# Scan products ahead of the output projection, one decay-difference pair on VectorE, and conv taps laid apart, in a Mamba-2 layer's step loop

## The chip, the cores and the metric

The kernel runs on one core of a Trainium2 chip. The metric is the time of one execution on the device in microseconds (us); lower is better. TensorE (PE, with PEld its weight loads), VectorE (DVE), ScalarE (ACT), GpSimd (POOL) and the DMA queue of SyncE (SP) run their own instruction streams in order and meet only at semaphores.

## The reference, cut to what matters

A decoder layer: a Mamba-2 block, then cross attention, then a mixture-of-experts block, each behind a LayerNorm. The change lies in the Mamba-2 block alone. Its input is 8 sequences of 256 tokens with 256 channels, and it has 64 heads of 64 channels (4096 inner channels).

```python
proj = x_normed @ W_in.T                 # z (4096), x (4096), B and C (128 each), dt (64)
xBC = silu(causal_conv(xBC, 4 taps) + conv_b)
dt = softplus(dt + dt_bias);  dA = dt * -exp(A_log)
# per head: decay from token s to token l is exp(cum_l - cum_s), cum being the running sum of dA
Y = sum over s <= l of (C_l . B_s) * exp(cum_l - cum_s) * dt_s * x_s
y = Y + D * x
g = y * silu(z);  out = rmsnorm(g) * norm_w @ W_out.T
```

## The kernel before

The tokens are cut into 4 groups of 512 (two sequences each, `BG` = 2), and the inner channels into 32 tiles of 128 (`NCT`), which hold two heads each (`HPT` = 2). A step `n` is one tile of one group: 128 steps (`N`), group by group. Each engine has a loop over the steps, written out by hand; there is no planner. While a group runs, the loops also prepare the next group (`prepare_next`: B, C, dt, the running sums, normalised and transposed tokens), a few instructions in most steps.

What one step does, with the lines of the profile:

- TensorE: `transposes(n)` turns the conv output (L1049), `x_proj(n + 2)` and `z_proj(n + 1)` project ahead, 6 products each (L1021), `prepare_next`, then `out_proj(n - 1)` (L1078) and `scan(n)` (L1062), the products of the masked decays with x dt. In the steps called `turned` (the second of a group, and the last), `scan(n)` stands ahead of `out_proj(n - 1)`.
- ScalarE, in this order: `scale_x(n + 1)` (conv tap 0 with bias, L503), `gaps(n + 2)` (L517 and L520: for each of 2 heads and 2 sequences, a 128x256 and a 128x128 activation that form max(cum - cum', 0) of a pair of rows; four pairs), `tanh_x(n + 1)` (L536), `square(n - 1)` (L532), `tanh_z(n + 1)` (L542), `prepare_next`, `decays(n + 2)` (the exponential of all differences, L526).
- VectorE: `gate(n - 1)` (L791, waits for the scan), `x_times_dt(n)` (L779, waits for the transposes), `conv_x(n + 1)` (L749: taps 1 to 3, each added to the same tile and each waiting for the one before; tap 1 waits for `scale_x(n + 1)`), `prepare_next`, `matrices(n + 1)` (L761), `silu_x(n + 1)` (L766), `silu_z(n + 1)` (L773).
- GpSimd: `matrices_off(n + 1)` (L387, after `matrices(n + 1)`), `product(n)` (L396, after `gate(n)`), `add_square(n - 1)` (L407). For the first 28 steps it also splits weights, `w_high(n + 4)` (L367) ahead of `product(n)` and `w_low(n + 4)` (L374) behind it.
- SP: `a_load(k + 5)` (running sums, broadcast to all partitions, L282), which waits for the gaps three steps earlier, then `w_load(k + 4)` (L265).

`tanh_x(n + 1)` waits for all taps of `conv_x(n + 1)`; what stands behind it on ScalarE waits with it, up to `scale_x(n + 2)` of the next round of the loop.

Of the kernel before, what the change touches and what calls it, by code (L numbers as in the profile page):

```python
# [9 lines left out]
ALU = mybir.AluOpType  # L10
ACT = mybir.ActivationFunctionType
AX_X = mybir.AxisListType.X

P = 128
# [6 lines left out]
TPG = TG // P  # L21
# [41 lines left out]
def mamba_phase(nc, xres, ident, raw, banks, scratch, tiny, xT, next_loads, keys, split, x, w_xz, w_bc, w_dt, conv_w, conv_b, dt_bias, a_log, d_param, norm_w,  # L63
# [5 lines left out]
    NCT = w_xz.shape[1]  # L69
    HD = 64  # L70
    HPT = P // HD
    NH = NCT * HPT
    CB = 2
    SEQ = 256
    BG = TG // SEQ
    TAPS = conv_w.shape[-1]
    CONV = TAPS - 1
    EPS = 1e-5
    N = NG * NCT
# [3 lines left out]
    EARLY = 2 * TPG  # L83
    WO_ACT = NCT - 12
    SOFT = 3 + len(LOG1P)
    numbers = []

    with ExitStack() as ctx:
# [3 lines left out]
        def sem(name):  # L92
            s = ctx.enter_context(nc.semaphore("m_" + name))
            numbers.append(s.num)
            return s
# [7 lines left out]
        cw = sb("cw", [P, conv_w.shape[1], TAPS])  # L103
# [5 lines left out]
        cum = sb("cum", [P, 2 * TPG, NH])  # L109
# [15 lines left out]
        a_all = [sb(f"a_all{u}", [P, HPT, TG])[:] for u in range(3)]  # L125
# [12 lines left out]
        late = raw[:, RING * XZ:]  # L138
# [3 lines left out]
        aT = late[:, (CB + 1) * TG:(CB + 1) * TG + SEQ]  # L142
# [9 lines left out]
        def pb(name, banks=1):  # L152
# [4 lines left out]
        ps_y, ps_s = pb("ps_y"), pb("ps_s")  # L157
# [25 lines left out]
            sem(n) for n in ("x_ready", "z_ready", "t_ready", "y_ready", "out_ready", "sum_ready"))  # L183
        (x_scaled, gap_done, exp_done, x_tanh, z_tanh, g_squared) = (
            sem(n) for n in ("x_scaled", "gap_done", "exp_done", "x_tanh", "z_tanh", "g_squared"))
        mat_off = sem("mat_off")
        (conv_step, x_silu, z_silu, xdt_done, mat_done, gy_done, g_done, sum_mean, x_added) = (
            sem(n) for n in ("conv_step", "x_silu", "z_silu", "xdt_done", "mat_done", "gy_done", "g_done",
                             "sum_mean", "x_added"))
# [36 lines left out]
        def first_rows(u, h, b):  # L226
            at = (h * BG + b) * 2 * P
            pair = mat[:, u, at:].rearrange("p (j t) -> p j t", t=P)
            step = (2 * HPT * BG * P + (h * BG + b) * P - at) // P
            return pair[:, 0:step + 1:step, :]  # L230

        def later_rows(u, h, b):
            at = (h * BG + b) * 2 * P + P
            return mat[:, u, at:at + P]

        block = ctx.enter_context(nc.Block())

        @block.sync
        def _(sp):
# [35 lines left out]
            def a_load(n):  # L275
                g, c, u = n // NCT, n % NCT, n % 3
                if n >= 3:
                    sp.wait_ge(gap_done, HPT * (n - 2))
                if c == 0:
                    sp.wait_ge(a_stored, 32 * (g + 1))  # L280
                row = a_dram[g, c * HPT:(c + 1) * HPT, :].rearrange("h t -> (h t)")
                sp.dma_start(a_all[u].rearrange("p h t -> p (h t)"), row.partition_broadcast(P))\  # L282
                    .then_inc(a_loaded[u], 16)
# [23 lines left out]
            for k in range(-2, N):  # L307
                g, j = k // NCT, k % NCT
# [144 lines left out]
        def _(act):  # L453
# [15 lines left out]
            def aT_copy(h):  # L469
                act.wait_ge(aT_ready, h + 1)  # L470
                if h >= 1:
                    act.wait_ge(a_stored, 32 * h)
                act.activation(aT[:], ps_s[:, 0:SEQ], ACT.Copy).then_inc(aT_done, 1)

            def bc_scale(h, i):
                m = h * CB + i
# [29 lines left out]
            def gaps(n, h):  # L506
                g, c, u = n // NCT, n % NCT, n % 3
                if h == 0:
                    act.wait_ge(a_loaded[u], 16 * (n // 3 + 1))
                    if c == 0:  # L510
                        act.wait_ge(cum_done, g + 1)
                    if n >= 3:
                        act.wait_ge(y_ready, n - 2)
                head = c * HPT + h
                for b in range(BG):
                    t = g % 2 * TPG + 2 * b
                    act.activation(first_rows(u, h, b),  # L517
                                   a_all[u][:, h, b * SEQ:(b + 1) * SEQ].rearrange("p (j t) -> p j t", t=P),
                                   ACT.Relu, bias=cum[:, t, head:head + 1], scale=-1.0)
                    last = act.activation(later_rows(u, h, b), a_all[u][:, h, b * SEQ + P:(b + 1) * SEQ],  # L520
                                          ACT.Relu, bias=cum[:, t + 1, head:head + 1], scale=-1.0)
                last.then_inc(gap_done, 1)

            def decays(n):
                act.wait_ge(gap_done, HPT * (n + 1))
                act.activation(mat[:, n % 3], mat[:, n % 3], ACT.Exp, scale=-1.0).then_inc(exp_done, 1)  # L526

            def square(n):
# [125 lines left out]
        def _(dve):  # L654
# [86 lines left out]
                dve.tensor_copy(cb_off[:, h % 2 * BG + b, :], ps_s[:, 2 * P:3 * P])  # L741
                dve.tensor_tensor(cb_diag[:, h % 2 * BG + b, :], ps_s[:, 0:2 * P], mask[:], ALU.mult).then_inc(cb_done, 1)

            def conv_x(n):
                c = n % NCT
                dve.wait_ge(x_scaled, n + 1)
                out, ps = batches(xc[:, n % 2, :]), batches(ps_x[n % 2][:, :])
                for k in range(1, TAPS):
                    dve.scalar_tensor_tensor(  # L749
                        out=out[:, :, k:], in0=ps[:, :, 0:SEQ - k],  # L750
                        scalar=cw[:, c, TAPS - 1 - k:TAPS - k], in1=out[:, :, k:],
                        op0=ALU.mult, op1=ALU.add).then_inc(conv_step, 1)
                    if k < TAPS - 1:
                        dve.wait_ge(conv_step, n * CONV + k)

            def matrices(n):
                g, diag = n // NCT % 2, diagonal(n % 3)
# [36 lines left out]
            def mean_out(g):  # L794
                dve.wait_ge(sum_ready, g + 1)
                dve.tensor_scalar(r_out[:], ps_s[:, 0:TPG], 1.0 / (NCT * P), None, ALU.mult).then_inc(sum_mean, 1)
# [78 lines left out]
                bc_taps_of(0, 1, k)  # L875
            bc_silu(0, 0)
            bc_silu(0, 1)
            conv_x(0)
            masked(0, 0)
            silu_x(0)  # L880
            masked(0, 1)
# [2 lines left out]
            silu_z(0)  # L884
            for n in range(N):
                turned = n % NCT == 1 and n > 1
                if n >= 1:
                    gate(n - 1)
                if turned:
                    mean_out(n // NCT - 1)  # L890
                if n >= 1:
                    x_times_dt(n)
                if n + 1 < N:
                    conv_x(n + 1)
                if turned:
                    add_out(n // NCT - 1)
                if n < N - NCT:
                    prepare_next(n)
                if n == 0:
                    silu_x(1)  # L900
                    matrices(1)
                    silu_z(1)
                elif n + 1 < N:
                    matrices(n + 1)
                    silu_x(n + 1)
                    silu_z(n + 1)
# [16 lines left out]
        def _(pe):  # L923
# [227 lines left out]
            for n in range(N):  # L1151
                if n >= 1:
                    transposes(n)
                if n + 2 < N:
                    x_proj(n + 2)
                if n + 1 < N:
                    z_proj(n + 1)
                if n < N - NCT:
                    prepare_next(n)
                if n == N - 1:  # L1160
                    context_keys(0)
                turned = n % NCT == 1 and n > 1 or n == N - 1
                if n >= 1 and not turned:
                    out_proj(n - 1)
                scan(n)
                if turned:
                    out_proj(n - 1)
                if n % NCT == 0 and n > 0:
                    sums(n // NCT - 1)
# [1560 lines left out]
```

## Time and profile before

| | |
|---|---|
| time, median of 3 runs | 1665.1 us (1664.83 to 1670.2) |
| span of the profiled execution, first to last instruction | 1663.1 us |
| median run over that span | 2.0 us |
| PE busy over the span | 1592.4 us (96%) |
| PE weight loads busy | 1281.1 us (77%) |
| DVE busy | 1248.2 us (75%) |
| ACT busy | 1202.6 us (72%) |
| POOL busy | 819.6 us (49%) |

Of the profiled execution its span is known; the median of the runs shown is 2.0 us above it. The step loop, from the first gate to the last, goes from 51.6 us to 918.2 us of the span; attention and experts follow.

How the rows of the section below are to be read. A row of a stretch has its length and then the busy us (and instructions) of PE, PEld, DVE, ACT and POOL, the granted clock of TensorE as a share of full speed, the DMA share and GB/s. A row of a timeline has the start and the length in us, the engine, line, operation, tiles and shapes, and in brackets the idle time of the engine ahead of it with what ended it; an instruction's length can overlap the start of the next one on its engine, so what an instruction takes of its engine's time is the distance of two starts. A row of a line has shortest, median and longest ns; a row of a group has its count, busy us and mean ns.

Busy time of PE contains modelled ends of overlapping products, so that a share near 100% says that products follow closely, not that none could be faster.

### The profile page before, as it was taken

What the parts mean: (1) busy time and instruction counts of PE and PEld (TensorE: products, weight loads), DVE (VectorE), ACT (ScalarE), POOL (GpSimd) and SP (SyncE); (2) the same over time, 40 slices, a digit from 0 to 9 for tenths busy, and PEclk for the clock granted to TensorE, in tenths of its full rate; (3) what the DMA queues carried; (4) which work ended last, traced back from release to release, by engine and by line L of the source; (5) the groups of instructions that cost most, each with busy time, mean ns of one, the idle gap of its engine ahead of it and who ended that gap; (6) DMA issues with size and microseconds to landing.
All of it is one profiled execution on the core that took longest, in us unless ns stands there. A gap on an engine that the chain in (4) does not pass through costs nothing. (4 is left out here: it accounts for less than half of the span.)

```text
span 1663.1 us, 29165 instructions
## 1 busy us (share of the span) xinstructions
PE 1592.4 (96%) x9876; PEld 1281.1 (77%) x9876; DVE 1248.2 (75%) x1954; ACT 1202.6 (72%) x2512; POOL 819.6 (49%) x673
## 2 busy tenths in 40 slices
PE   4999999999999999999999999999969999999999
PEld 3777777777777777777777667877758889999888
DVE  6899999999898999998899656766566534433355
ACT  5999899999999999999999566766624334443331
POOL 5677786555555555555565422211124563335460
PEclk8999999999999999999999999999979999999999
DMA  7555555444444454464442100000215333222231
GB/s 283 187 173 176 188 177 165 152 149 156 156 160 145 152 166 167 154 247 154 170 158 89 57 1 14 14 14 27 96 67 178 128 108 108 93 93 93 78 100 52
DMA packets 76239, 209.85 MB, mean 126 GB/s; under 512 B 9152, under 2 KB 32960, under 8 KB 74304
## 3 DMA queue, kind: packets, MB, share of 16 engines
q1 hardware_dynamic: 70432, 181.90, 32.1%
q0 software_dynamic: 5664, 26.09, 4.5%
q8 instruction: 85, 1.39, 0.3%
q14 instruction: 58, 0.48, 0.1%
HBM read 170.99 MB, written 36.96 MB: 125 GB/s over the span
## 5 line engine op out<-in xcount | busy, mean ns | idle before, releaser
L1021 PE MATMUL banks<-pair_hi,m_wxz 128*128 128x512 f32 x1024 | 352.4, 405 | 3.8 <-DVE pair_lo L674 2.3
L749 DVE SCALAR_TENSOR_TENSOR m_xc<-banks,m_cw,m_xc 128x510 f32<-128x510 f32 (+2 forms) x384 | 285.7, 744 | 12.5 <-ACT m_xc L503 2.6
L387 POOL TENSOR_TENSOR m_mat<-m_mat,m_cb_off 128x512 f32<-128x512 f32 x128 | 166.4, 1300 | 220.4 <-DVE m_mat L761 211.4
L517 ACT ACTIVATE m_mat<-m_a_all,m_cum 128x256 f32<-128x256 f32 x512 | 260.0, 508 | 1.6 <-PE m_ps_y L1062 1.6
L1078 PE MATMUL m_ps_out<-m_won,m_gT 128*128 128x256 f32 x1024 | 242.6, 379 | 4.8 <-POOL m_gT L396 3.3
L1021 PEld LDWEIGHTS banks<-pair_hi,m_wxz 128*128 128x128 f32 x1024 | 194.0, 189 | 42.6 <-issue 2.7
L396 POOL TENSOR_TENSOR m_gT<-m_gy,m_zs 128x512 f32<-128x512 f32 x128 | 166.9, 1304 | 106.5 <-DVE m_gy L791 106.2
L1078 PEld LDWEIGHTS m_ps_out<-m_won,m_gT 128*128 128x128 f32 x1024 | 191.7, 189 | 35.8 <-POOL m_gT L396 5.4
L520 ACT ACTIVATE m_mat<-m_a_all,m_cum 128x128 f32<-128x128 f32 x512 | 204.5, 399 | 0.0
L1021 PE MATMUL banks<-pair_lo,m_wxz 128*128 128x512 f32 x512 | 201.1, 393 | 0.0
L1062 PE MATMUL m_ps_y<-m_mat,m_xdt 128*64 128x256 f32 (+1 forms) x2048 | 194.7, 332 | 0.0
L526 ACT ACTIVATE m_mat<-m_mat 128x1536 f32<-128x1536 f32 x128 | 189.6, 1481 | 0.1
L1062 PEld LDWEIGHTS m_ps_y<-m_mat,m_xdt 128*64 128x64 f32 x2048 | 126.8, 136 | 80.0 <-issue 42.2
L761 DVE TENSOR_TENSOR m_mat<-m_mat,m_cb_diag 128x1024 f32<-128x1024 f32 x128 | 165.6, 1294 | 0.3 <-ACT m_mat L526 0.3
L407 POOL TENSOR_TENSOR m_g_sum<-m_g_sum,m_g_sq 128x512 f32<-128x512 f32 x124 | 162.8, 1313 | 5.2 <-ACT m_g_sq L532 5.1
L2571 PE MATMUL f_gu<-f_room,f_gT_hi 128*128 x468 | 141.3, 363 | 2.4 <-issue 2.4
L2430 DVE TENSOR_TENSOR f_h<-f_silu,f_gu 128x256 f32<-128x256 f32 (+1 forms) x117 | 44.1, 377 | 129.5 <-PE f_ps_hT L2581 104.1
L791 DVE SCALAR_TENSOR_TENSOR m_gy<-m_xs,logits,m_ps_y 128x512 f32<-128x512 f32 x128 | 95.3, 745 | 42.0 <-PE m_ps_y L1062 41.6
L1362 POOL TENSOR_TENSOR a_q_r<-a_q_ve,a_neg_half 128x32 f32<-128x32 f32 x8 | 43.4, 5427 | 168.9 <-DVE a_q_ve L1555 168.9
L1021 PEld LDWEIGHTS banks<-pair_lo,m_wxz 128*128 128x128 f32 x512 | 97.4, 190 | 16.3
L2496 PE MATMUL f_gu<-pair_hi,f_room 128*128 128x512 f32 x320 | 103.7, 401 | 6.3 <-DVE f_room L2251 6.3
L2213 ACT ACTIVATE f_silu<-f_gu 128x256 f32<-128x256 f32 (+1 forms) x117 | 40.7, 348 | 88.3 <-PE f_gu L2571 88.3
(350 smaller groups left out, 3432.3 us busy)
## 6 DMA issues: line engine op xcount, KB each, us to landing
m_a_all<-a_by_head SPq DMA_DIRECT2D x128, 512.0 KB, 4.0
m_wxz<-w_split SPq DMA_DIRECT2D x96, 512.0 KB, 4.8
w_split<-m_wxz SPq DMA_DIRECT2D x32, 512.0 KB, 3.0
raw<-in_w_gate_up POOLq DMA_DIRECT2D x9, 1280.0 KB, 6.7
raw<-in_w_xz SPq DMA_DIRECT2D x32, 256.0 KB, 4.0
raw<-in_w_down POOLq DMA_DIRECT2D x9, 640.0 KB, 7.7
x_sorted<-f_gT_hi SPq DMA_DIRECT2D x1, 4992.0 KB, 16.2
f_xg<-x_sorted SPq DMA_DIRECT2D x39, 128.0 KB, 2.3
```

The costliest lines, as they stand in the source:

```text
L387: pool.tensor_tensor(off, off, cb_off[:, g * BG:(g + 1) * BG, :].rearrange("p b t -> p (b t)").unsqueeze(1) .broadcast_to([P, HPT, BG * P] ...
L396: pool.tensor_tensor(gT[:, n % 2, :], gy[:, n % 2, :], zs[:, n % 2, :], ALU.mult).then_inc(g_done, 1)
L407: pool.tensor_tensor(g_sum[:, g % 2, :], g_sum[:, g % 2, :], g_sq[:, n % 2, :], ALU.add)\
L517: act.activation(first_rows(u, h, b), a_all[u][:, h, b * SEQ:(b + 1) * SEQ].rearrange("p (j t) -> p j t", t=P), ACT.Relu, bias=cum[:, t, h ...
L520: last = act.activation(later_rows(u, h, b), a_all[u][:, h, b * SEQ + P:(b + 1) * SEQ], ACT.Relu, bias=cum[:, t + 1, head:head + 1], scale ...
L526: act.activation(mat[:, n % 3], mat[:, n % 3], ACT.Exp, scale=-1.0).then_inc(exp_done, 1)
L749: dve.scalar_tensor_tensor(out=out[:, :, k:], in0=ps[:, :, 0:SEQ - k], scalar=cw[:, c, TAPS - 1 - k:TAPS - k], in1=out[:, :, k:], op0=ALU. ...
L761: dve.tensor_tensor(diag, diag, cb_diag[:, g * BG:(g + 1) * BG, :].rearrange("p b t -> p (b t)").unsqueeze(1) .broadcast_to([P, HPT, BG * ...
L1021: last = pe.matmul(ps[:, :], w, a, start=m == 0, stop=m == len(terms) - 1)
L1062: last = pe.matmul(ps_y[h * HD:(h + 1) * HD, b * SEQ + at:(b + 1) * SEQ], xdt[:, 2 * b + half, h * HD:(h + 1) * HD], later_rows(u, h, b) i ...
L1078: last = pe.matmul(ps_out[:, q * HID:(q + 1) * HID], gT[:, n % 2, q * P:(q + 1) * P], won[:, c, :], start=c == 0 and q % 2 == 0, stop=c == ...
L2571: last = pe.matmul(ps_gu[m % 4][:, 0:2 * (i1 - i0)], a, w, start=q == 0, stop=q == len(terms) - 1)
```

## The change

On TensorE `scan(n)` now stands ahead of `out_proj(n - 1)` in every step. On VectorE a new function `gap(n)` forms one of the four pairs of decay differences (head 1, sequence 1) with two `tensor_scalar` instructions (add the running sum, maximum with 0), where ScalarE formed it with two activations; a new semaphore `gap_dve_done` tells `decays` and `a_load`. The sign that the activations applied (`scale=-1.0`) moves into the copy `aT_copy`, once a group. The three taps of `conv_x(n + 1)` are called one by one: tap 1 between `gate(n - 1)` and `x_times_dt(n)`, tap 2 behind `x_times_dt(n)`, then `gap(n + 2)`, `add_out` and `prepare_next(n)`, and tap 3 behind these.

```diff
--- before.py
+++ after.py
@@ -83,6 +83,7 @@
     EARLY = 2 * TPG
     WO_ACT = NCT - 12
     SOFT = 3 + len(LOG1P)
+    GAP_DVE = (1, 1)
     numbers = []
 
     with ExitStack() as ctx:
@@ -183,7 +184,7 @@
             sem(n) for n in ("x_ready", "z_ready", "t_ready", "y_ready", "out_ready", "sum_ready"))
         (x_scaled, gap_done, exp_done, x_tanh, z_tanh, g_squared) = (
             sem(n) for n in ("x_scaled", "gap_done", "exp_done", "x_tanh", "z_tanh", "g_squared"))
-        mat_off = sem("mat_off")
+        mat_off, gap_dve_done = sem("mat_off"), sem("gap_dve_done")
         (conv_step, x_silu, z_silu, xdt_done, mat_done, gy_done, g_done, sum_mean, x_added) = (
             sem(n) for n in ("conv_step", "x_silu", "z_silu", "xdt_done", "mat_done", "gy_done", "g_done",
                              "sum_mean", "x_added"))
@@ -232,6 +233,13 @@
         def later_rows(u, h, b):
             at = (h * BG + b) * 2 * P + P
             return mat[:, u, at:at + P]
+
+        def gap_parts(n, h, b):
+            g, u, head = n // NCT, n % 3, n % NCT * HPT + h
+            t = g % 2 * TPG + 2 * b
+            return (a_all[u][:, h, b * SEQ:(b + 1) * SEQ].rearrange("p (j t) -> p j t", t=P),
+                    cum[:, t, head:head + 1], a_all[u][:, h, b * SEQ + P:(b + 1) * SEQ],
+                    cum[:, t + 1, head:head + 1])
 
         block = ctx.enter_context(nc.Block())
 
@@ -276,6 +284,7 @@
                 g, c, u = n // NCT, n % NCT, n % 3
                 if n >= 3:
                     sp.wait_ge(gap_done, HPT * (n - 2))
+                    sp.wait_ge(gap_dve_done, n - 2)
                 if c == 0:
                     sp.wait_ge(a_stored, 32 * (g + 1))
                 row = a_dram[g, c * HPT:(c + 1) * HPT, :].rearrange("h t -> (h t)")
@@ -470,7 +479,7 @@
                 act.wait_ge(aT_ready, h + 1)
                 if h >= 1:
                     act.wait_ge(a_stored, 32 * h)
-                act.activation(aT[:], ps_s[:, 0:SEQ], ACT.Copy).then_inc(aT_done, 1)
+                act.activation(aT[:], ps_s[:, 0:SEQ], ACT.Copy, scale=-1.0).then_inc(aT_done, 1)
 
             def bc_scale(h, i):
                 m = h * CB + i
@@ -511,18 +520,17 @@
                         act.wait_ge(cum_done, g + 1)
                     if n >= 3:
                         act.wait_ge(y_ready, n - 2)
-                head = c * HPT + h
                 for b in range(BG):
-                    t = g % 2 * TPG + 2 * b
-                    act.activation(first_rows(u, h, b),
-                                   a_all[u][:, h, b * SEQ:(b + 1) * SEQ].rearrange("p (j t) -> p j t", t=P),
-                                   ACT.Relu, bias=cum[:, t, head:head + 1], scale=-1.0)
-                    last = act.activation(later_rows(u, h, b), a_all[u][:, h, b * SEQ + P:(b + 1) * SEQ],
-                                          ACT.Relu, bias=cum[:, t + 1, head:head + 1], scale=-1.0)
+                    if (h, b) == GAP_DVE:
+                        continue
+                    rows, first, late, later = gap_parts(n, h, b)
+                    act.activation(first_rows(u, h, b), rows, ACT.Relu, bias=first)
+                    last = act.activation(later_rows(u, h, b), late, ACT.Relu, bias=later)
                 last.then_inc(gap_done, 1)
 
             def decays(n):
                 act.wait_ge(gap_done, HPT * (n + 1))
+                act.wait_ge(gap_dve_done, n + 1)
                 act.activation(mat[:, n % 3], mat[:, n % 3], ACT.Exp, scale=-1.0).then_inc(exp_done, 1)
 
             def square(n):
@@ -741,17 +749,28 @@
                 dve.tensor_copy(cb_off[:, h % 2 * BG + b, :], ps_s[:, 2 * P:3 * P])
                 dve.tensor_tensor(cb_diag[:, h % 2 * BG + b, :], ps_s[:, 0:2 * P], mask[:], ALU.mult).then_inc(cb_done, 1)
 
-            def conv_x(n):
+            def conv_x(n, k):
                 c = n % NCT
-                dve.wait_ge(x_scaled, n + 1)
+                if k == 1:
+                    dve.wait_ge(x_scaled, n + 1)
+                else:
+                    dve.wait_ge(conv_step, n * CONV + k - 1)
                 out, ps = batches(xc[:, n % 2, :]), batches(ps_x[n % 2][:, :])
-                for k in range(1, TAPS):
-                    dve.scalar_tensor_tensor(
-                        out=out[:, :, k:], in0=ps[:, :, 0:SEQ - k],
-                        scalar=cw[:, c, TAPS - 1 - k:TAPS - k], in1=out[:, :, k:],
-                        op0=ALU.mult, op1=ALU.add).then_inc(conv_step, 1)
-                    if k < TAPS - 1:
-                        dve.wait_ge(conv_step, n * CONV + k)
+                dve.scalar_tensor_tensor(
+                    out=out[:, :, k:], in0=ps[:, :, 0:SEQ - k],
+                    scalar=cw[:, c, TAPS - 1 - k:TAPS - k], in1=out[:, :, k:],
+                    op0=ALU.mult, op1=ALU.add).then_inc(conv_step, 1)
+
+            def gap(n):
+                u = n % 3
+                dve.wait_ge(a_loaded[u], 16 * (n // 3 + 1))
+                if n % NCT == 0:
+                    dve.wait_ge(cum_done, n // NCT + 1)
+                if n >= 3:
+                    dve.wait_ge(y_ready, n - 2)
+                rows, first, late, later = gap_parts(n, *GAP_DVE)
+                dve.tensor_scalar(first_rows(u, *GAP_DVE), rows, first, 0.0, ALU.add, ALU.max)
+                dve.tensor_scalar(later_rows(u, *GAP_DVE), late, later, 0.0, ALU.add, ALU.max).then_inc(gap_dve_done, 1)
 
             def matrices(n):
                 g, diag = n // NCT % 2, diagonal(n % 3)
@@ -875,7 +894,10 @@
                 bc_taps_of(0, 1, k)
             bc_silu(0, 0)
             bc_silu(0, 1)
-            conv_x(0)
+            for k in range(1, TAPS):
+                conv_x(0, k)
+            gap(0)
+            gap(1)
             masked(0, 0)
             silu_x(0)
             masked(0, 1)
@@ -884,23 +906,30 @@
             silu_z(0)
             for n in range(N):
                 turned = n % NCT == 1 and n > 1
+                more = n + 1 < N
                 if n >= 1:
                     gate(n - 1)
                 if turned:
                     mean_out(n // NCT - 1)
+                if more:
+                    conv_x(n + 1, 1)
                 if n >= 1:
                     x_times_dt(n)
-                if n + 1 < N:
-                    conv_x(n + 1)
+                if more:
+                    conv_x(n + 1, 2)
+                if n + 2 < N:
+                    gap(n + 2)
                 if turned:
                     add_out(n // NCT - 1)
                 if n < N - NCT:
                     prepare_next(n)
+                if more:
+                    conv_x(n + 1, 3)
                 if n == 0:
                     silu_x(1)
                     matrices(1)
                     silu_z(1)
-                elif n + 1 < N:
+                elif more:
                     matrices(n + 1)
                     silu_x(n + 1)
                     silu_z(n + 1)
@@ -1159,11 +1188,8 @@
                     prepare_next(n)
                 if n == N - 1:
                     context_keys(0)
-                turned = n % NCT == 1 and n > 1 or n == N - 1
-                if n >= 1 and not turned:
-                    out_proj(n - 1)
                 scan(n)
-                if turned:
+                if n >= 1:
                     out_proj(n - 1)
                 if n % NCT == 0 and n > 0:
                     sums(n // NCT - 1)
```

## Rows read from the trace of the kernel before

**Rows 1.** Busy time by engine in four stretches, one for each token group.

```profile
52.00:281.00 229.00, 216.62 (x1324) 167.60 (x1322) 222.75 (x296) 215.22 (x438) 175.65 (x157) 1.00 0.53 179
281.00:500.00 219.00, 217.06 (x1332) 169.09 (x1331) 202.53 (x300) 211.53 (x434) 124.91 (x103) 1.00 0.46 154
500.00:717.00 217.00, 216.53 (x1331) 169.24 (x1331) 200.76 (x289) 209.73 (x427) 123.87 (x99) 1.00 0.46 157
717.00:918.00 201.00, 198.78 (x1223) 153.24 (x1222) 180.94 (x248) 192.78 (x384) 117.42 (x94) 1.00 0.47 161
```

**Rows 2.** Timeline of one plain step of the last group, PE left out.

```profile
824.07 0.75 DVE L791 SCALAR_TENSOR_TENSOR m_gy<-m_xs,logits,m_ps_y 128x512 f32<-128x512 f32 x1 [0.56 <-PE m_ps_y L1062]
824.74 0.68 DVE L779 TENSOR_TENSOR m_xdt<-banks,m_dt 128x512 f32<-128x512 f32 x1
...
825.34 2.30 DVE L749 SCALAR_TENSOR_TENSOR m_xc<-banks,m_cw,m_xc 128x510 f32<-128x510 f32 x3
...
826.15 1.30 POOL L407 TENSOR_TENSOR m_g_sum<-m_g_sum,m_g_sq 128x512 f32<-128x512 f32 x1
...
827.55 1.22 DVE L761 TENSOR_TENSOR m_mat<-m_mat,m_cb_diag 128x1024 f32<-128x1024 f32 x1
...
827.67 0.60 ACT L536 ACTIVATE banks<-m_xc 128x512 f32<-128x512 f32 x1
...
828.73 0.58 ACT L542 ACTIVATE xn_ffn<-banks 128x512 f32<-128x512 f32 x1
...
829.21 1.47 ACT L526 ACTIVATE m_mat<-m_mat 128x1536 f32<-128x1536 f32 x1
829.34 0.69 DVE L773 SCALAR_TENSOR_TENSOR m_zs<-xn_ffn,banks 128x512 f32<-128x512 f32 x1
...
830.58 0.77 ACT L503 ACTIVATE m_xc<-banks,logits,m_cw 128x512 f32<-128x512 f32 x1
830.59 0.75 DVE L791 SCALAR_TENSOR_TENSOR m_gy<-m_xs,logits,m_ps_y 128x512 f32<-128x512 f32 x1 [0.56 <-PE m_ps_y L1062]
```

**Rows 3.** Timeline of weight loads: a plain step, a turned step, the last step.

```profile
829.02 1.28 PEld L1062 LDWEIGHTS m_ps_y<-m_mat,m_xdt 128*64 128x64 f32 x16 [0.33 <-issue]
...
504.01 1.28 PEld L1062 LDWEIGHTS m_ps_y<-m_mat,m_xdt 128*64 128x64 f32 x16 [0.35 <-issue]
...
918.13 1.59 PEld L1078 LDWEIGHTS m_ps_out<-m_won,m_gT 128*128 128x128 f32 x8 [0.17 <-issue]
```

**Rows 4.** Lines L668 and L853, all their instructions: shortest, median, longest ns.

```profile
L668 DVE TENSOR_SCALAR xn_ffn<-xres,m_mv,m_rstd x8: 382/409/1483, 9.5 to 21.0; 128x256 f32<-128x256 f32 x8
...
L853 DVE TENSOR_SCALAR m_cw<-m_cw x1: 220/220/220, 14.5 to 14.5; 128x136 f32<-128x136 f32 x1
```

**Rows 5.** Timelines of VectorE and GpSimd around one such instruction.

```profile
11.09 0.45 POOL L356 TENSOR_TENSOR m_wdt_hl<-xn_ffn,m_wdt_hl 128x128 fp32r<-128x128 f32 x1
...
11.44 1.48 DVE L668 TENSOR_SCALAR xn_ffn<-xres,m_mv,m_rstd 128x256 f32<-128x256 f32 x1
11.50 1.26 POOL L358 TENSOR_TENSOR m_wbc_lo<-raw,m_wbc_hi 128x512 fp32r<-128x512 f32 x1
```

**Rows 6.** Timeline of an early step, in which GpSimd also splits weights.

```profile
163.03 0.74 DVE L791 SCALAR_TENSOR_TENSOR m_gy<-m_xs,logits,m_ps_y 128x512 f32<-128x512 f32 x1
...
165.11 1.30 POOL L374 TENSOR_TENSOR m_wxz<-raw,m_wxz 128x512 fp32r<-128x512 f32 x1
...
166.36 1.28 POOL L407 TENSOR_TENSOR m_g_sum<-m_g_sum,m_g_sq 128x512 f32<-128x512 f32 x1
```

**Rows 7.** Groups by line, second token group: first and last preparing lines, DVE and ACT.

```profile
L727 DVE SCALAR_TENSOR_TENSOR raw<-xn_ffn,m_cw,raw 128x510 f32<-128x510 f32 (+2 forms) x6 | 4.4, 739 | 0.0
...
L698 DVE TENSOR_SCALAR xn_ffn<-raw 128x256 f32<-128x256 f32 x1 | 0.3, 284 | 0.0
...
L553 ACT ACTIVATE xn_ffn<-xres,m_mv,m_rstd 128x256 f32<-128x256 f32 x4 | 2.3, 640 | 0.0
...
L473 ACT ACTIVATE raw<-m_ps_s 128x256 f32<-128x256 f32 x1 | 0.4, 371 | 0.0
```

## The prediction

> **What bounds the kernel now.** I read the table of stretches first, then the timeline of one plain step, then the places where VectorE and GpSimd run together. The four stretches of the step loop are 229, 219, 217 and 201 us for 32, 32, 32 and 31 steps, with PE, DVE and ACT all above 90% of the second and third and TensorE's granted clock at 1.00 [rows 1]. Three engines are nearly full, so no single share tells what holds a step.
>
> The timeline does. In a plain step, one that prepares nothing, gate follows gate by 830.59 - 824.07 = 6.52 us, and the gate sits idle for 0.56 us until TensorE's scan is done [rows 2]. TensorE has no such wait: what stands ahead of its scan is 0.33 us of issue, in steps of any length [rows 3]. So TensorE's 6.52 us set the plain step, and DVE has 0.56 us to spare. A second thing is nearly as long, and the reader should see it as a loop through two engines: `tanh_x` waits for the taps of `conv_x`, ScalarE then works in order down to `scale_x` of the next round, and that lets the next taps start. From the start of `tanh_x` (827.67) to the start of `scale_x` (830.58) are 2.91 us, `scale_x` lasts 0.77, the taps 2.30 [rows 2]; the taps ended at 827.64, so a hand-over is 0.03, and there are two. Sum: 2.91 + 0.77 + 2.30 + 0.06 = 6.04 us a round, 0.48 below TensorE's 6.52.
>
> **The change part by part.** *Scan ahead of the output projection.* No product is added. Where the trace has the new neighbours, the scan behind projections idles 0.35 us and the output projection behind a scan 0.17, against 0.33 for the scan in the old place [rows 3]. TensorE's step grows by 0.02 at the least and 0.19 at the most, to 6.54 to 6.71. The gate's 0.56 us of waiting goes; what is late next is not on TensorE.
>
> *Taps apart.* Tap 1 still needs `scale_x`, and `tanh_x` still needs tap 3, so all that now stands between them enters the loop. Price by distances of starts: a tap 0.67 (as the gate, 824.07 to 824.74, the same operation on 512 columns), `x_times_dt` 0.60 (824.74 to 825.34), a second tap 0.67, the new pair, and the last tap 0.75 to its end [rows 2].
>
> *The pair on VectorE.* No row shows this operation with these scalars. The nearest are a `tensor_scalar` of 128x256 with two per-partition scalars, 0.38 us at the shortest, and one of 128x136 with a constant, 0.22 [rows 4]. Together 0.60; each overlaps its follower by some 0.07 as the gate does (0.75 long, 0.67 apart, rounded), so I take 0.46. From below: twice the 0.22, less overlap, 0.30. From above: 384 columns cost no more than the 0.68 of a 512-column operation [rows 2] plus a second instruction's 0.22, less overlap, 0.76.
>
> VectorE's part of the loop is then 0.67 + 0.60 + 0.67 + 0.46 + 0.75 = 3.15 instead of 2.30, and the loop 2.91 + 0.77 + 0.06 + 3.15 = **6.89 us**, longer than TensorE's step. That is the forecast's core: the taps save two semaphore waits, but they stretch a round trip that had only 0.48 us to spare.
>
> *Two activations fewer on ScalarE.* `gaps` lies between `scale_x` and `tanh_x`, where ScalarE will wait for tap 3: four pairs fitted into about 6.52 - 2.91 - 0.67 = 2.9 us, three need 2.2, and the room becomes 6.89 - 2.91 - 0.67 = 3.3. The relief turns into about 1.1 us of idleness a step and gains nothing. Without that cover it would be worth some 0.7 us a step.
>
> *Preparation.* `prepare_next` on VectorE now stands ahead of tap 3, and ScalarE's stands between `tanh_z` and `decays`; both are in the loop and add in full. In the second group VectorE's are fifteen lines from 4.4 to 0.3 us, 42 instructions, 18.4 us in sum; ScalarE's eight lines from 2.3 to 0.4 us, 17 instructions, 9.2 us [rows 7]. Less overlaps (0.07 and about 0.09 each) 15.5 and 7.7 us. The third group lacks the normalising and the turned tokens: 12.9 and 4.7 us. The first lacks `add_out`: 14.1 us of VectorE.
>
> *The shared path of VectorE and GpSimd.* The row at 11.44 is a `tensor_scalar` that needs 0.38 and took 1.48: it began under one GpSimd operation (11.09 to 11.54), and a second (11.50 to 12.76) followed at once; it ended only behind both [rows 5]. So the pair waits for a run of GpSimd operations that follow each other closely. Where does it fall? Counted from `tanh_x`: `matrices` starts 0.12 earlier, `silu_z` 1.79 after that, the gate 0.62 later, at 2.29; tap 1 at 2.91 + 0.77 + 0.03 = 3.71; the pair 1.94 later, at 5.65. GpSimd's `add_square` begins 2.08 after the gate and lasts 1.30 [rows 2], so ends at 5.67. In plain steps the pair comes just as GpSimd falls silent: cost 0.02, taken as nothing. In the first 28 steps GpSimd also has `w_low`, 2.08 to 3.38 behind the gate, and then `add_square` until 4.61 [rows 6], at 6.90 of my count: the pair waits 1.25 us. ScalarE's preparation there only shortens that wait.
>
> The Trainium skill (SBUF — State Buffer, Who interferes with whom) says that a `tensor_scalar` in a two-port mode and a GpSimd instruction exclude each other for a whole instruction and that the earlier to issue wins. The trace agrees on the exclusion (1.48 us for 0.38). If the pair had issued ahead of `add_square`, the rule would spare the early steps their 1.25 us; what that would give is rival one.
>
> *Nothing else.* The sign in `aT_copy` costs no instruction. `a_load` on SP newly waits for the pair, with `w_load` queued behind it; those weights are used two rounds later, over 6 us after the pair, so between nothing and a short wait: taken as nothing. `decays` waits for the pair too, but stands behind `tanh_x`, hence behind tap 3, which follows the pair: nothing. The two calls ahead of the loop cost up to 3 us; taken as nothing.
>
> **Sum.** First group: 28 x (6.89 + 1.25) + 4 x 6.89 + 14.1 = 269.6, against 229: +40.6. Second: 32 x 6.89 + 15.5 + 7.7 = 243.7, against 219: +24.7. Third: 220.5 + 12.9 + 4.7 = 238.1, against 217: +21.1. Last: 29 whole steps by 6.89 - 6.52: +10.7. Together +97.1 us. On the profiled span of 1663.1 this is 1760; the median of the runs shown is 2.0 above the span, so **1762 us**.
>
> **The rivals.** *One, the pair never meets GpSimd* (its offset differs by some tenths, or the operation doesn't use the shared path). The first group is then 32 x 6.89 + 14.1 + 7.7 = 242.3, which is 27.3 less: 1735 us. For it: the offsets are close to the edge in plain steps. Against: in early steps GpSimd is busy for 3.8 us on end behind the gate.
>
> *Two, the pair meets `add_square` in plain steps as well.* This decides as soon as the gate comes later than 2.29 on my count, or GpSimd lags. Half a microsecond in 99 further steps makes 50: 1812 us. Against: the gate no longer waits for the scan.
>
> *Three, separating the taps saves nothing on VectorE*, because an operation must drain before the next begins whether or not a wait stands between. Then the three taps and their neighbours keep the distance (0.77) that (2.30 - 0.75)/2 gives for waiting taps [rows 2], 0.2 us more in the loop, 127 x 0.2 = 25: 1787 us. Against it speaks the gate, 0.67 to its follower with the same number of columns.
> The Trainium skill (VectorE: DVE Perf Modes, The DRAIN you can't avoid) states this rule, that chaining without semaphores is no faster; the row of the gate differs from it by 0.1 us, and the row decides.
>
> *Four, on the other side: the loop doesn't bind and TensorE sets every step.* The first group's excess over 32 x 6.52 (20.4 us) falls to the third's (8.4), where ScalarE and VectorE hold least, and the second's 10.4 likewise: 14 less, plus 127 x 0.02 for the order: 1654 us. It decides if the loop is below 6.54, that is, if VectorE's part takes under 2.8 instead of 3.15; three taps and `x_times_dt` alone are 2.69, which leaves the pair 0.1, and no preparation could stand in the loop.
>
> **How the numbers follow.** Forecast 0.62, rival one 0.18, two 0.06, three 0.05, four 0.09. About 0.3%, 5 us, is what a measurement can tell from no change: within rival four I put 0.05 on faster, 0.03 on none and 0.01 on slower, so faster 0.05, same 0.03, slower 0.92. The pair's bounds move the forecast by 127 x -0.16 = -20 and 127 x 0.30 = +38. The range goes from below rival one (1735, less half the lower bound) to the upper bound: 1725 to 1800. It leaves out rivals two and four.
>
> **What would show each step.** Right: plain steps of about 6.9 us; tap 1 idle for `scale_x` some 0.7 us a step and `tanh_x` idle for tap 3 about 1.1; the gate hardly waits for the scan; TensorE's busy share of the loop falls; the pair's 256-column half averages above 1.3 us in the first 28 steps and near 0.4 later. Wrong: plain steps near 6.5 with the gate still waiting for TensorE; or `tanh_x` never idle. The forecast fails low if the early pair doesn't stall, and high if it stalls throughout.

## The result and the profile after

The changed kernel takes 1755.0 us (median, 1754.1 to 1757.0) against 1665.0 us before: a ratio of 1.0538, 95% interval 1.0524 to 1.0552. It is slower by 90 us; 1762 was forecast. The span of the profiled execution is 1755.2 us, 92.1 more than before.

The table of stretches of the changed kernel, cut at the gates of steps 0, 32, 64, 96 and 127 (columns as in [rows 1]):

```profile
54.00:317.00 263.00, 223.82 (x1319) 166.30 (x1317) 233.65 (x361) 192.55 (x372) 174.56 (x156) 1.00 0.46 155
317.00:560.00 243.00, 224.68 (x1334) 168.88 (x1334) 212.84 (x363) 191.13 (x370) 125.85 (x103) 1.00 0.43 139
560.00:798.00 238.00, 223.79 (x1327) 167.83 (x1327) 210.90 (x354) 188.76 (x362) 123.60 (x100) 1.00 0.44 143
798.00:1010.00 212.00, 207.55 (x1227) 153.85 (x1228) 189.28 (x307) 173.66 (x327) 117.94 (x94) 0.99 0.45 153
```

The four stretches were 229, 219, 217 and 201 us. Everything that was lost is lost here: 34, 24, 21 and 11 us, and 2.5 us ahead of the first gate (54.1 instead of 51.6). In [rows 1] PE, DVE and ACT were nearly full in the second stretch; now PE is busy for 92% of it, VectorE for 88% and ScalarE for 79%. Work was moved from ScalarE, little was added, and all three engines are emptier, though the stretch is longer: no engine is busy throughout. What sets it is a round trip through two engines, as the next rows show.

One plain step of the last group, in the timeline of the changed kernel:

```profile
883.44 0.74 DVE L810 SCALAR_TENSOR_TENSOR m_gy<-m_xs,logits,m_ps_y 128x512 f32<-128x512 f32 x1
...
884.88 0.75 DVE L759 SCALAR_TENSOR_TENSOR m_xc<-banks,m_cw,m_xc 128x510 f32<-128x510 f32 x1 [0.70 <-ACT m_xc L512]
...
885.51 1.29 POOL L416 TENSOR_TENSOR m_g_sum<-m_g_sum,m_g_sq 128x512 f32<-128x512 f32 x1
885.54 0.68 DVE L798 TENSOR_TENSOR m_xdt<-banks,m_dt 128x512 f32<-128x512 f32 x1
...
886.14 0.74 DVE L759 SCALAR_TENSOR_TENSOR m_xc<-banks,m_cw,m_xc 128x508 f32<-128x508 f32 x1
...
886.80 0.35 DVE L772 TENSOR_SCALAR m_mat<-m_a_all,m_cum 128x256 f32<-128x256 f32 x1
887.06 0.28 DVE L773 TENSOR_SCALAR m_mat<-m_a_all,m_cum 128x128 f32<-128x128 f32 x1
887.25 0.74 DVE L759 SCALAR_TENSOR_TENSOR m_xc<-banks,m_cw,m_xc 128x506 f32<-128x506 f32 x1
...
888.02 0.60 ACT L544 ACTIVATE banks<-m_xc 128x512 f32<-128x512 f32 x1 [1.11 <-DVE m_xc L759]
...
890.30 0.74 DVE L810 SCALAR_TENSOR_TENSOR m_gy<-m_xs,logits,m_ps_y 128x512 f32<-128x512 f32 x1
890.93 0.77 ACT L512 ACTIVATE m_xc<-banks,logits,m_cw 128x512 f32<-128x512 f32 x1
```

Read it as a circle. `tanh_x` (L544) begins at 888.02, 0.03 behind the end of tap 3. ScalarE reaches `scale_x` (L512) 2.91 us later, tap 1 idles 0.70 us for it, and then tap 1, `x_times_dt`, tap 2, the pair and tap 3 follow each other without a gap. Gate follows gate by 6.86 us. The 0.56 us by which the gate waited for TensorE [rows 2] are gone; in their place tap 1 waits 0.70 us for ScalarE and `tanh_x` 1.11 us for VectorE. Each engine waits for the other once a round.

An early step of the same kernel, VectorE and GpSimd:

```profile
200.11 1.30 POOL L383 TENSOR_TENSOR m_wxz<-raw,m_wxz 128x512 fp32r<-128x512 f32 x1
...
201.36 1.27 POOL L416 TENSOR_TENSOR m_g_sum<-m_g_sum,m_g_sq 128x512 f32<-128x512 f32 x1
201.39 1.39 DVE L772 TENSOR_SCALAR m_mat<-m_a_all,m_cum 128x256 f32<-128x256 f32 x1
```

The pair's first half takes 1.39 us here and 0.35 in the plain step: it starts 0.03 us after `add_square` has started and waits for it, though the program has no semaphore between the two.

### The profile page after: what moved, and what is told of

Read it like the earlier page. It is cut to its first block and busy times, and to the rows that moved or that the text cites. A ratio compares the mean times of both kernels' runs of the same rounds, so it can differ in the third digit from the quotient of the medians.

```text
span 1755.2 us, 29541 instructions
## 1 busy us (share of the span) xinstructions
PE 1622.2 (92%) x9876; PEld 1278.7 (73%) x9876; DVE 1289.2 (73%) x2210; ACT 1117.1 (64%) x2256; POOL 818.1 (47%) x673
## 3 DMA queue, kind: packets, MB, share of 16 engines
q8 instruction: 85, 1.39, 0.3%
## 5 line engine op out<-in xcount | busy, mean ns | idle before, releaser
L1107 PE MATMUL m_ps_out<-m_won,m_gT 128*128 128x256 f32 x1024 | 255.3, 393 | 1.8 <-POOL m_gT L405 1.8
L1107 PEld LDWEIGHTS m_ps_out<-m_won,m_gT 128*128 128x128 f32 x1024 | 184.5, 190 | 43.8 <-issue 21.8
L544 ACT ACTIVATE banks<-m_xc 128x512 f32<-128x512 f32 x128 | 77.0, 602 | 210.2 <-DVE m_xc L759 210.2
L1050 PE MATMUL banks<-pair_lo,m_wxz 128*128 128x512 f32 x512 | 201.7, 394 | 0.0
L527 ACT ACTIVATE m_mat<-m_a_all,m_cum 128x256 f32<-128x256 f32 x384 | 192.9, 502 | 0.0
L780 DVE TENSOR_TENSOR m_mat<-m_mat,m_cb_diag 128x1024 f32<-128x1024 f32 x128 | 155.8, 1217 | 0.0
L528 ACT ACTIVATE m_mat<-m_a_all,m_cum 128x128 f32<-128x128 f32 x384 | 151.5, 394 | 0.0
L1078 PE MATMUL banks<-ident,m_xs 128*128 128x128 f32 x512 | 83.3, 286 | 59.7 <-DVE m_xs L785 58.2
L1078 PEld LDWEIGHTS banks<-ident,m_xs 128*128 128x128 f32 x512 | 55.7, 142 | 103.0 <-DVE m_xs L785 101.2
```

The costliest lines, as they stand in the source:

```text
L527: act.activation(first_rows(u, h, b), rows, ACT.Relu, bias=first)
L780: dve.tensor_tensor(diag, diag, cb_diag[:, g * BG:(g + 1) * BG, :].rearrange("p b t -> p (b t)").unsqueeze(1) .broadcast_to([P, HPT, BG * ...
L1050: last = pe.matmul(ps[:, :], w, a, start=m == 0, stop=m == len(terms) - 1)
L1107: last = pe.matmul(ps_out[:, q * HID:(q + 1) * HID], gT[:, n % 2, q * P:(q + 1) * P], won[:, c, :], start=c == 0 and q % 2 == 0, stop=c == ...
```

## The experiments

The theory: the step is the round trip `tanh_x`, `decays`, `scale_x`, taps; VectorE's instructions between tap 1 and tap 3 are in it, and so is any wait of the pair for GpSimd. Rivals: the order on TensorE, the pair as work of VectorE, or the taps' separation costs the time in itself.

Median times, the five parts of the step loop (distances of the gates of steps 0, 32, 64, 96, 127) and the plain step near the end of the loop, all in us:

| kernel | time | first | second | third | last | plain step |
|---|---|---|---|---|---|---|
| before | 1665.0 | 228.8 | 219.5 | 216.6 | 201.7 | 6.52 |
| changed | 1755.0 | 262.8 | 243.2 | 237.6 | 212.2 | 6.86 |
| order alone | 1667.8 | 229.4 | 219.8 | 217.7 | 203.1 | 6.55 |
| taps alone | 1699.5 | 238.8 | 230.1 | 225.6 | 207.0 | 6.52 |
| pair alone, behind the taps | 1691.0 | 240.8 | 222.8 | 221.2 | 205.5 | 6.52 |
| changed, pair on ScalarE | 1697.1 | 238.8 | 230.0 | 225.0 | 205.7 | 6.55 |
| changed, preparation behind | 1731.1 | 258.0 | 232.5 | 229.9 | 211.2 | 6.86 |
| changed, pair and preparation behind | 1685.9 | 240.3 | 222.2 | 219.3 | 206.1 | 6.55 |
| changed, short squares early | 1734.7 | 242.4 | 243.3 | 237.7 | 210.8 | 6.86 |
| changed, pair late | 1730.9 | 240.1 | 243.3 | 237.6 | 212.2 | 6.86 |
| changed, square ahead | 1720.7 | 256.6 | 231.6 | 227.1 | 205.0 | 6.62 |
| the same, short squares | 1685.2 | 230.4 | 227.3 | 223.4 | 205.8 | 6.55 |
| pair late, taps together, old order | 1676.9 | 228.9 | 222.9 | 221.2 | 205.3 | 6.52 |

### The three parts one by one

**The order alone**, on the kernel before:

```diff
-                turned = n % NCT == 1 and n > 1 or n == N - 1
-                if n >= 1 and not turned:
-                    out_proj(n - 1)
                 scan(n)
-                if turned:
+                if n >= 1:
                     out_proj(n - 1)
```

> The kernel before with the new order on TensorE alone: scan ahead of the output projection in every step. Theory (the loop tanh_x, decays, scale_x, taps sets the changed kernel's step): this loop stays at 6.04 us, TensorE keeps setting the plain step, which grows from 6.52 by 0.02 to 0.06 us: 1668 to 1673 us. Rival (the scan, called earlier, waits for xdt or the matrices, and this costs the time): plain steps near 6.8, 1700 us or more.

1667.8 us, just under the range, ratio 1.0015 (1.0006 to 1.0024), plain steps 6.55. The weight loads of this kernel show the two neighbours that [rows 3] had promised, from a turned and from the last step:

```profile
883.04 1.28 PEld L1062 LDWEIGHTS m_ps_y<-m_mat,m_xdt 128*64 128x64 f32 x16 [0.35 <-issue]
884.49 1.59 PEld L1078 LDWEIGHTS m_ps_out<-m_won,m_gT 128*128 128x128 f32 x8 [0.17 <-issue]
```

The order costs 0.03 us a step and no wait for data; the rival falls.

**The taps alone**, with `add_out` and the preparation between taps 2 and 3:

```diff
+                if more:
+                    conv_x(n + 1, 1)
                 if n >= 1:
                     x_times_dt(n)
-                if n + 1 < N:
-                    conv_x(n + 1)
+                if more:
+                    conv_x(n + 1, 2)
                 if turned:
                     add_out(n // NCT - 1)
                 if n < N - NCT:
                     prepare_next(n)
+                if more:
+                    conv_x(n + 1, 3)
```

> The kernel before with the taps laid apart alone (add_out and the preparation between taps 2 and 3), pair on ScalarE, old order on TensorE. Theory: the loop becomes 6.43 us, under TensorE's 6.52, so plain steps stay at 6.52; steps with preparation take 6.43 plus the preparation of VectorE and ScalarE, second token group about 229 us instead of 219.5: 1677 to 1687 us in all. Rival (taps apart save two waits a step and cost nothing): 1655 to 1663 us.

1699.5 us, above what the theory gave. The plain step stayed at 6.52 and the second group came to 230.1, as expected, but the theory's loop of 6.43 us was summed wrongly. Nothing stands between taps 2 and 3 in a plain step, so tap 3 still waits for tap 2 and starts 0.77 us behind it; tap 1 to tap 3's end is 2.78 us, and the loop 2.91 + 0.77 + 0.03 + 2.78 + 0.03 = 6.52 us: as long as TensorE's step, with nothing to spare. What I had missed besides is in the first group (238.8): the preparation's instructions are slower there (its conv taps, which read two tiles, average 1368 ns; 738 in the second group), and that time is now in the loop too. That they wait for GpSimd's early work fits the run with the pair late, below; no run tests it apart. Of the last group's 5.3 us more, 4.5 lie in one step, in which TensorE waits for weights for 3.8 us instead of 1.8. In the second group tap 1 idles for `scale_x`, which it hardly did before:

```profile
DVE m_xc L757 <- ACT m_xc L511: 26.3, 30, 1.7
```

(sum of the waits, their number, the longest). One wait between taps was saved in a plain step, and the kernel lost 2%.

**The pair alone**, behind three taps that stay together, old order:

```diff
                 if n >= 1:
                     x_times_dt(n)
-                if n + 1 < N:
-                    conv_x(n + 1)
+                if more:
+                    conv_x(n + 1, 1)
+                    conv_x(n + 1, 2)
+                    conv_x(n + 1, 3)
+                if n + 2 < N:
+                    gap(n + 2)
                 if turned:
                     add_out(n // NCT - 1)
```

> The kernel before with the pair on VectorE alone, placed behind the three taps, taps together behind x_times_dt, old order on TensorE. Theory: the pair is outside the loop (6.04 us), plain steps stay at 6.52 us; in the first 28 steps the pair starts about 3.5 us behind the gate, under add_square, which ends at 4.61, and VectorE, which sets those steps, is longer by 0.46 to 1.5 us: 1680 to 1710 us. Rival (the pair itself is the cost wherever it stands): plain steps near 6.9, 1720 us or more.

1691.0 us, plain steps 6.52. Nearly half of the loss is in the first group, where the pair's first half averages 1229 ns, again under GpSimd:

```profile
L772 DVE TENSOR_SCALAR m_mat<-m_a_all,m_cum 128x256 f32<-128x256 f32 x28 | 34.4, 1229 | 0.0
```

Alone, the parts cost 3.0, 34.7 and 26.1 us, 63.8 together; the whole change costs 90.1. What is missing comes of the pair standing between the taps; the next run shows it.

**The changed kernel without the pair**, which ScalarE forms again:

```diff
-    GAP_DVE = (1, 1)
+    GAP_DVE = None
...
-                if n + 2 < N:
-                    gap(n + 2)
```

> The changed kernel with the pair given back to ScalarE: taps apart and the new order on TensorE stay. Theory: loop 6.43 us plus preparation, no waiting for GpSimd in the first 28 steps, plain steps near TensorE's 6.55: 1678 to 1695 us. Rival (the taps' separation or TensorE's order holds the step at 6.86): 1740 us or more.

1697.1 us, just above the range; the first group is again the part that I had too low, and the loop is again 6.52 us and not 6.43, so that TensorE's 6.55 leave it 0.02. Order and taps together cost 32.3 us, 5.4 less than one by one. Adding the pair between the taps to this kernel costs 57.9 us, more than twice what it costs behind the taps of the kernel before (26.1).

### What stands between the taps

**Only the preparation moved** behind tap 3 of the changed kernel, then **the pair as well**:

```diff
                 if more:
                     conv_x(n + 1, 2)
+                    conv_x(n + 1, 3)
                 if n + 2 < N:
                     gap(n + 2)
                 if turned:
                     add_out(n // NCT - 1)
                 if n < N - NCT:
                     prepare_next(n)
-                if more:
-                    conv_x(n + 1, 3)
```

(this is the second; in the first, tap 3 stands behind `gap`).

> The changed kernel with add_out and VectorE's preparation moved behind tap 3; the pair stays between taps 2 and 3. Theory: plain steps stay at 6.86 us; the preparation leaves the loop and falls into VectorE's 0.7 us of waiting for scale_x, 14.1, 15.5 and 12.9 us in the three groups, less what exceeds 0.7 us in one step: 1712 to 1725 us. Rival (VectorE's own sum of work sets the preparing steps): about 1755 us.

> The changed kernel with tap 3 directly behind tap 2: the pair, add_out and the preparation all behind the taps. Theory: loop 6.4 us, plain steps at TensorE's 6.55 us; in the first 28 steps the pair begins under add_square and VectorE's own work sets the step at 7.5 to 8 us, first group about 250 us: 1680 to 1700 us in all. Rival (VectorE's longer list of work is the cost, not its place): plain steps stay near 6.86, 1740 us or more.

The first gave 1731.1 us: 23.9 better, where 30 to 43 were expected. Plain steps stayed at 6.86, and the second group fell by 10.7 of 15.5 us. Of the 29.1 us that VectorE waited for `scale_x` in that group 16.3 remain, so 12.8 were filled; tap 1 waits in 24 of the 32 steps instead of 31, and in the others VectorE's own work has become the longer part. The second gave 1685.9 us with plain steps at 6.55 (the first group, 240.3, was expected at about 250): without the pair the circle is 6.52, and the step is TensorE's again, by 0.02 us. The same list of instructions on VectorE, with one instruction in another place, is 45 us faster than the other.

### GpSimd and the pair

**Short squares**: the changed kernel with 4 columns in `add_square` of the first 28 steps.

```diff
+                    cols = 4 if n < 28 else TG
-                    pool.tensor_tensor(g_sum[:, g % 2, :], g_sum[:, g % 2, :], g_sq[:, n % 2, :], ALU.add)\
+                    pool.tensor_tensor(g_sum[:, g % 2, 0:cols], g_sum[:, g % 2, 0:cols], g_sq[:, n % 2, 0:cols], ALU.add)\
```

> The changed kernel, in which add_square adds 4 of 512 columns in the first 28 steps (this leaves out most of the sum of squares of those tiles). Theory: the pair no longer waits for GpSimd behind w_low; the 1.05 us a step vanish, and ScalarE's preparation of 7.7 us, hidden by that wait, comes back: 1726 to 1736 us, the pair's 256-column half near 0.35 us throughout. Rival (the pair is slow in the early steps for another reason): 1753 to 1757 us, the half still near 1.39.

1734.7 us, 20 less, all in the first group (262.8 to 242.4). The same place in the timeline:

```profile
198.56 0.20 POOL L417 TENSOR_TENSOR m_g_sum<-m_g_sum,m_g_sq 128x4 f32<-128x4 f32 x1
198.59 0.34 DVE L773 TENSOR_SCALAR m_mat<-m_a_all,m_cum 128x256 f32<-128x256 f32 x1
```

Nothing but GpSimd's work was changed, and the pair is at its 0.34 us.

**The pair late**: the changed kernel, whose pair is formed by ScalarE in the first token group.

```diff
+    GAP_FROM = 32
...
-                    if (h, b) == GAP_DVE:
+                    if (h, b) == GAP_DVE and n >= GAP_FROM:
                         continue
```

> The changed kernel with the pair on ScalarE for the steps of the first token group and on VectorE afterwards. Theory: the first group falls from 262.8 to about 230 us, the others stay at 243, 238 and 212: 1715 to 1726 us. Rival (the early steps are held by VectorE's and GpSimd's own work): first group above 250, 1743 us or more.

1730.9 us, first group 240.1: the theory's 230 was too low, for the reason met twice above. The groups by line of its first 28 steps show who took over the wait, `matrices` and the preparation's taps:

```profile
L783 DVE TENSOR_TENSOR m_mat<-m_mat,m_cb_diag 128x1024 f32<-128x1024 f32 x28 | 40.6, 1448 | 0.0
...
L738 DVE SCALAR_TENSOR_TENSOR raw<-xn_ffn,m_cw,raw 128x510 f32<-128x510 f32 (+2 forms) x6 | 8.2, 1370 | 0.0
```

In the changed kernel they average 1210 and 735 ns: there the pair had waited for GpSimd ahead of them. So of the pair's wait a part had been paid already by others.

**Square ahead**: ScalarE's `square(n - 1)` ahead of `tanh_x(n + 1)`; then the same with short squares in all steps.

```diff
+                if 1 <= n < N - 1:
+                    square(n - 1)
                 if n + 1 < N:
                     tanh_x(n + 1)
                 if n == N - 1:
                     wq_high()
-                if n >= 1:
                     square(n - 1)
```

> The changed kernel with ScalarE's square(n - 1) moved ahead of tanh_x(n + 1), where ScalarE idles 1.1 us a plain step; this takes 0.52 us out of the loop. Theory with GpSimd's lock as a second limit: the pair now comes 0.5 us ahead of the end of add_square, waits for it, and gives the 0.52 us back; plain steps stay within 0.05 of 6.86 us, the pair's 256-column half rises from 0.35 to about 0.85 us in them: 1742 to 1756 us in all. Rival (the loop alone decides): plain steps fall to TensorE's 6.55 us, 1700 to 1715 us.

> As the run before, and add_square adds 4 of 512 columns in all steps (this leaves out most of the sum of squares). Theory: with both limits gone the loop is about 6.34 us, plain steps fall to TensorE's 6.55 us, the pair's half stays near 0.35: 1680 to 1700 us. Rival (the separated taps, the pair or the order cost the time in themselves): plain steps stay near 6.86, 1730 us or more.

The first gave 1720.7 us and plain steps of 6.62, between the theory's 6.86 and the rival's 6.55; its total fits neither. The pair's wait is there, but smaller than I had it:

```profile
886.13 1.30 POOL L416 TENSOR_TENSOR m_g_sum<-m_g_sum,m_g_sq 128x512 f32<-128x512 f32 x1
...
886.96 0.62 DVE L773 TENSOR_SCALAR m_mat<-m_a_all,m_cum 128x256 f32<-128x256 f32 x1
```

0.62 - 0.35 = 0.27 us are given back of the 0.52 taken out: 6.86 - 0.52 + 0.27 = 6.61. With short squares the wait goes, plain steps are TensorE's 6.55, and the time is 1685.2 us, as expected. Both limits are real; the wait was mis-sized.

### Can ScalarE's relief be had otherwise?

**The pair late, taps together, old order**: the pair behind the taps as above, from step 32 on.

> The kernel before with the pair on VectorE behind the three taps from the second token group on, and on ScalarE in the first; old order on TensorE, taps together. Theory: the first group stays at 229 us, the others at 223, 221 and 205 as where the pair stands behind the taps throughout: 1670 to 1679 us, no faster than the kernel before. Rival (relieving ScalarE pays where GpSimd splits no weights): 1655 to 1662 us.

1676.9 us, ratio 1.0072 (1.0055 to 1.0089): slower than before. The stretch of its second group:

```profile
280.00:503.00 223.00, 218.17 (x1338) 169.60 (x1334) 215.75 (x364) 191.81 (x370) 126.35 (x104) 1.00 0.45 152
```

VectorE is busy for 97% of it (92% in [rows 1]) and ScalarE for 86%. Plain steps keep TensorE's 6.52; in steps that prepare, VectorE has become the longest. 3.2 of the last group's 3.6 us of loss lie in one step, in which TensorE waits for a load of weights for 3.4 us instead of 1.8. Why that load comes later is open.

No version here beats the kernel before.

## Why the prediction was right

- **What bounded the kernel before.** TensorE's 6.52 us in plain steps: right. With the order alone they are 6.55, and every version whose loop is short returns to 6.52 or 6.55. With the taps apart and the pair elsewhere the loop is 6.52 itself, so those three versions show TensorE's bound less clearly than the others.
- **The loop of 6.89 us.** Measured 6.86. ScalarE's 2.91 and 0.77 are unchanged, tap 1 to tap 3's end is 887.25 + 0.74 - 884.88 = 3.11 instead of 3.15.
- **The pair's 0.46.** From 886.80 to 887.25 it takes 0.45; the bounds, 0.30 and 0.76, were not needed.
- **ScalarE's relief gains nothing.** `tanh_x` idles 1.11 us, as forecast (1.1), tap 1 0.70 (0.7).
- **Preparation in the loop.** Second and third group: +23.7 and +21.0 measured, +24.7 and +21.1 forecast. The last group: +10.5 for +10.7. Moving VectorE's preparation out shows that it was in the loop; ScalarE's was not moved, and its 7.7 and 4.7 us rest on the sums.
- **The early wait.** The mechanism was right, the size was off: in steps in which ScalarE prepares nothing, the first few apart, the half takes 1.39 us, so the wait is 1.39 - 0.35 = 1.04 us instead of 1.25. The term "28 x (6.89 + 1.25)" is therefore 5.9 us too high, which is most of the first group's 6.6 (+34.0 measured, +40.6 forecast). I counted to the recorded end of `add_square`, but the pair ends 0.15 us behind it and needs 0.35, so it was let go about 0.20 us ahead of that end; the row at 11.44 had shown the same (it ends at 12.92, GpSimd's operation at 12.76, it needs 0.38) [rows 5].
- **One sign failed.** The half was to average above 1.3 us in the first 28 steps. It averages 1.09:

```profile
L772 DVE TENSOR_SCALAR m_mat<-m_a_all,m_cum 128x256 f32<-128x256 f32 x28 | 30.5, 1089 | 0.0
```

In steps in which ScalarE prepares, the pair comes later under `add_square` and takes 0.42 to 1.12 us. The prediction had said so ("only shortens that wait") and set the sign without it. The sum stands all the same: 28 x (1.09 - 0.35) = 20.7 us of waiting and ScalarE's 7.7 make 28.4, close to 28 x 1.04 = 29.1.

- **The calls ahead of the loop** were taken as nothing with a bound of 3 us. The first gate came 2.5 us later here; over the runs with these calls it came 1.0 to 2.7 us later, over those without them between 0.2 earlier and 0.9 later, so that not all of the 2.5 is shown to be theirs.
- **The rivals.** One (the pair never meets GpSimd) falls with the 1.39 us. Two (it meets `add_square` in plain steps too) does not happen here, but 0.5 us earlier it does, as the run with the square ahead shows. Three falls: tap 2 and its follower stand 886.80 - 886.14 = 0.66 us apart, against 0.77 for waiting taps. The Trainium skill (VectorE: DVE Perf Modes, The DRAIN you can't avoid) has it from a row of copies that chaining without semaphores is no faster, though it also lets an instruction that is not held start earlier. Here a follower that need not wait for the tap ahead of it starts 0.11 us sooner, and the measurement decides. Four falls with the loop.

The steps sum to 34.0 + 23.7 + 21.0 + 10.5 + 2.5 = 91.7 of the span's 92.1 us. The forecast of 97.1 had 7.9 us too much in the four groups and 2.5 too little ahead of them: its total came a little closer than its terms, and that part is luck.

## What to carry to other kernels

Before laying a dependent series of instructions apart, follow the value that it makes around to its own next input: if another engine works on it in order and feeds the series again, all that is put in between lengthens that circle, and full engines hide how little room it had (0.48 us here). An engine that gets emptier without the step getting shorter is the sign of it. Moved work costs nothing only if its new place is in no circle, beside no user of a shared path, and on an engine with room in every step: 0.6 us of pair cost 58 us of the kernel between the taps, 26 behind them, and still 11.5 behind them from the second token group on.

## What the runs showed of the hardware

- A `tensor_scalar` on VectorE that starts during a GpSimd operation on 512 columns waits for it, with no semaphore between them (1.39 us for 0.35 at 201.39 in the changed kernel, 0.62 for 0.35 at 886.96 with the square ahead). In each of the changed kernel's 25 such waits of more than 0.15 us it ends 0.15 us behind the recorded end of that operation, however late it came. As it needs 0.35, it seems to be let go about 0.20 us ahead of that recorded end. The Trainium skill (SBUF — State Buffer, Who interferes with whom) has the later of the two wait until the earlier is through; the trace agrees, with the recorded end of GpSimd as an upper bound for that moment.
- Behind a GpSimd operation on 4 columns, recorded as 0.20 us, the same instruction started 0.03 us later and took 0.34 us: no wait at all.
- A conv tap that waits for the tap directly ahead of it starts 0.77 to 0.79 us after that tap's start (kernel before, taps alone); an instruction that has no such wait starts 0.66 us after it (changed kernel). The tap itself is recorded with 0.74 us.
